# Gate folded into the FFN weights, first batch's keys taken raw out of PSUM, and new engine orders

## The reference

```
mod = silu(c) @ wmod                      # six vectors a batch: sa ca ga sb cb gb
ga, gb = sign * max(|.|, 0.25)
h = layernorm(x) * (1 + ca) + sa
q, k, v = h @ Wqkv + bqkv                 # 256 wide each, one head
x = x + ga * (softmax(q k^T / 16) v @ Wo + bo)
h = layernorm(x) * (1 + cb) + sb
W = weight + lora_B[b] @ lora_A[b]        # combined for each batch
x = x + gb * (h @ W^T + bias)
```

## Time and profile before

| | |
|---|---|
| median of three runs | 1043.1 us |
| the profiled execution, its own time | 1042.57 us |
| its span, first to last instruction | 1040.8 us |
| PE busy | 1011.5 us, 97% |
| DVE, ACT, POOL busy | 663.6, 309.2, 231.2 us |
| mean granted TensorE clock | 0.993 of full |
| read from and written to HBM | 146.25 MB and 33.65 MB |

### The profile page before, as it was taken

The page is one execution under the profiler, slowest core; times in us unless marked ns, Lnnn a source line. Parts: engine busy times, 40 slices in busy tenths (PEclk is TensorE's granted clock), DMA queues, the critical chain, the costliest instruction groups (busy, mean ns, idle before and its releaser), DMA issues.

```text
span 1040.8 us, 12891 instructions
## 1 busy us (share of the span) xinstructions
PE 1011.5 (97%) x5158; PEld 831.6 (80%) x5158; DVE 663.6 (64%) x827; ACT 309.2 (30%) x460; POOL 231.2 (22%) x182
## 2 busy tenths in 40 slices
PE   4899999999999999999999999999999999999996
PEld 1677777888888889888898888888887888888885
DVE  4866756498744398532976548776688578566622
ACT  1422333123232132420234523322432333142300
POOL 0000000423201322004230034342223315042411
PEclk9899999999999999999999999999999999999999
DMA  9987574767102553024443146565553646463421
GB/s 348 409 317 244 211 295 140 252 227 265 70 1 77 207 197 127 1 94 157 155 162 117 41 142 225 203 220 184 200 202 126 216 145 202 140 225 122 142 76 66
DMA packets 54475, 180.74 MB, mean 174 GB/s; under 512 B 5784, under 2 KB 6352, under 8 KB 54416
## 3 DMA queue, kind: packets, MB, share of 16 engines
q1 hardware_dynamic: 45152, 146.35, 40.9%
q0 software_dynamic: 9104, 33.04, 8.4%
q10 hardware_dynamic: 160, 0.53, 0.1%
HBM read 146.25 MB, written 33.65 MB: 173 GB/s over the span
## 4 chain that ended last, share of the span: by engine, by line
PE 91%; DMA 4%; DVE 2%; SPq 1%; issue 1%; POOL 0%; ACT 0%; DVEq 0%; POOLq 0%; ACTq 0%
PE pairC L1370 8%; PE pairA L1370 8%; PE pairC L1371 8%; PE pairC L1372 7%; PE pairA L1371 7%; PE pairA L1372 7%; PE pairD L1370 7%; PE pairD L1371 7%; PE pairD L1372 7%; PE pairB L1370 5%; PE pairB L1371 5%; PE pairB L1372 5%; DMA z_cols<-in_x_cols 2%; PE pairB L1526 1%; PE pairD L1478 1%; PE pairA L1478 1%
## 5 line engine op out<-in xcount | busy, mean ns | idle before, releaser
L923 POOL TENSOR_TENSOR xr<-xr,row_bc 128x1024 f32<-128x1024 f32 x32 | 79.9, 2503 | 110.1 <-DMA xr<-in_x 90.3
L936 POOL TENSOR_TENSOR res<-res,row_bc 128x1024 f32<-128x1024 f32 x32 | 81.7, 2565 | 83.4 <-DMA res<-x_dram 76.9
L1370 PE MATMUL pairC<-w_hi,h_hi 128*128 128x512 f32 (+1 forms) x256 | 90.1, 352 | 0.0
L1371 PE MATMUL pairC<-w_lo,h_hi 128*128 128x512 f32 (+1 forms) x256 | 90.0, 351 | 0.0
L1372 PE MATMUL pairC<-w_hi,h_lo 128*128 128x512 f32 (+1 forms) x256 | 89.6, 350 | 0.0
L1370 PE MATMUL pairD<-w_hi,h_hi 128*128 128x512 f32 (+1 forms) x224 | 77.6, 346 | 0.0
L1371 PE MATMUL pairD<-w_lo,h_hi 128*128 128x512 f32 (+1 forms) x224 | 77.6, 346 | 0.0
L1372 PE MATMUL pairD<-w_hi,h_lo 128*128 128x512 f32 (+1 forms) x224 | 77.2, 345 | 0.0
L928 POOL DMA_DIRECT2D x_dram<-xr x32 | 18.0, 562 | 229.3 <-DVE xr L1276 229.3
L1079 ACT ACTIVATE w_hi<-w_sum 128x1024 fp32r<-128x1024 f32 x32 | 33.8, 1059 | 100.5 <-DVE w_sum L1320 100.2
L1370 PE MATMUL pairB<-w_hi,h_hi 128*128 128x512 f32 (+1 forms) x160 | 59.8, 374 | 0.0
(11 more groups left out here) (344 smaller groups left out, 2570.9 us busy)
## 6 DMA issues: line engine op xcount, KB each, us to landing
wm<-in_wmod SPq DMA_DIRECT2D x48, 512.0 KB, 6.4
xr<-in_x SPq DMA_DIRECT2D x34, 512.0 KB, 4.0
z_cols<-in_x_cols SPq DMA_DIRECT2D x32, 512.0 KB, 6.3
x_dram<-xr POOLq DMA_DIRECT2D x32, 512.0 KB, 3.8
xs<-x_dram SPq DMA_DIRECT2D x32, 512.0 KB, 4.7
w2t<-in_w2t SPq DMA_DIRECT2D x32, 512.0 KB, 4.3
res<-x_dram SPq DMA_DIRECT2D x32, 512.0 KB, 5.7
out_y<-res POOLq DMA_DIRECT2D x31, 512.0 KB, 3.5
```

Source lines behind the costliest of these rows:

```text
L923: nc.gpsimd.tensor_tensor(xt, xt, row_bc[:, :], ALU.add).then_inc(residual_made, 1)
L936: nc.gpsimd.tensor_tensor(rt, rt, row, ALU.add).then_inc(residual2_made, 1)
L1370: nc.tensor.matmul(out, left[0], right[0], start=first, stop=False)
L1371: nc.tensor.matmul(out, left[0], right[1], start=False, stop=False)
```

## The change

Four things are changed.

1. The gate gb is multiplied into the combined weights: a new step `WG` (DVE) multiplies each piece of `w_sum` by the gate in place, between `WS` and `WH2`. `FG` and the buffer `gated` are gone; `FA` adds the PSUM pair straight to `res`, and it is `FA` that frees the pair.
2. The product for the first vector, ca, is cut by output columns and no longer by rows: `M0`, `MC0`, `MT0`, `MM0`, each for two column tiles of h. Each of its eight loads brings 256 columns of 512 rows, in pieces of 1 KB where a whole row of 4 KB was one piece. A new step `V0` makes values in chunks as `K0` does keys.
3. The spread statistics are taken for both halves of the first batch by PE (`BCM` the means, `BCP` the rest), and ACT copies them out of PSUM (`BMC`, `BPC`) into `bc`, where `Z` reads them; before, the second half went through DRAM.
4. Keys of the first batch are copied raw out of PSUM into `k_raw` (`KR`, ACT), and `KH` and `KL` read that. `k_raw` lies where wm tiles lay, so that the second vector's loads have four tiles in turn, not six.

All five tables are new. The core of the diff:

```
-PARTS = ((1, 0), (1, 1), (0, 0), (0, 1), (2, 0), (2, 1))
+PARTS = ((1, 0), (2, 0), (1, 1), (2, 1), (0, 0), (0, 1))
 PE_ORDER:
-    ("BCP", (), "A", None), ("M", (0, 0), "B", None), ("M", (0, 1), "B", None), ("M", (0, 2), "B", None),
+    ("BCM", (0,), "A", None), ("BCP", (0,), "A", None), ("M0", (0,), "B", None), ("MT0", (0,), "B", None),
...
-            elif what == "BCP":
-                eng.wait_ge(z_made, 4)
+            elif what == "BCM":
+                eng.wait_ge(spread_copied, 2 * i[0] + 2)
+            elif what == "K" and i[0] == 0:
+                eng.wait_ge(k_raw_made, 2 * i[1] + 2)
-                eng.wait_ge(y_gated, f_no(*i) + 1)
+                eng.wait_ge(y_made, f_no(*i) + 1)
...
+                    if s == CA:
+                        half, at = k % 2, q * H + k // 2 * 2 * P
+                        src = wmod[half * BANK:(half + 1) * BANK, at:at + 2 * P].rearrange("(k p) n -> p k n", p=P)
+                        sp.dma_start(wm[k].rearrange("p (k n) -> p k n", k=4), src).then_inc(ld_wm[k], 16)
...
+                elif what in ("BMC", "BPC"):
+                    j = i[0]
+                    wait(act, z_made, 4 * j)
+                    nc.scalar.activation(bc[:, cols], ps[:, cols], ACT.Copy).then_inc(spread_copied, 1)
+                elif what == "KR":
+                    _, j, m = i
+                    act.wait_ge(k_done, 2 * j + m + 1)
+                    act.wait_ge(mod_used, 6)
+                    nc.scalar.activation(k_raw[:, m, j * CHUNK:(j + 1) * CHUNK], ps[:, m * BANK:(m + 1) * BANK],
+                                         ACT.Copy).then_inc(k_raw_made, 1)
...
                 elif what == "WH2":
-                    act.wait_ge(w_sum_made, 8 * b + n + 1)
+                    act.wait_ge(w_gated, 8 * b + n + 1)
...
+                elif what == "MM0":
+                    c = i[0]
+                    dve.wait_ge(ca_turned, c + 1)
+                    nc.vector.tensor_scalar(modT[:, PLACE[CA], :, 2 * c:2 * c + 2],
+                                            ps[:, BANK:BANK + 2 * B].rearrange("p (c b) -> p b c", b=B), 1.0, None,
+                                            ALU.add).then_inc(ca_made, 1)
...
-                elif what == "FG":
+                elif what == "WG":
+                    b, n = i
+                    h = n // 4
+                    dve.wait_ge(ld_gate2, 16 * (b + 1))
+                    dve.wait_ge(w_sum_made, 8 * b + n + 1)
+                    wt = w_sum[:, n % 2, :].rearrange("p (c n) -> p c n", c=2)
+                    gate = gate_bc[:, h * BANK:(h + 1) * BANK].unsqueeze(1).to_broadcast([P, 2, BANK])
+                    nc.vector.tensor_tensor(wt, wt, gate, ALU.mult).then_inc(w_gated, 1)
+                elif what == "FA":
+                    dve.wait_ge(residual2_made, n + 1)
-                            nc.vector.tensor_tensor(gated[:, cols], ps[:, cols], gate_bc[:, BANK:2 * BANK],
-                                                    ALU.mult).then_inc(y_half_gated, 1)
-                            nc.vector.tensor_tensor(res[:, slot, cols], res[:, slot, cols], gated[:, cols],
+                            nc.vector.tensor_tensor(res[:, slot, cols], res[:, slot, cols], ps[:, cols],
                                                     ALU.add).then_inc(y_half_made, 1)
                     dve.wait_ge(f_done, n + 1)
-                    gate = gate_bc[:, h * BANK:(h + 1) * BANK].unsqueeze(1).to_broadcast([P, 2, BANK])
-                    nc.vector.tensor_tensor(gated[:, :].rearrange("p (t n) -> p t n", t=2),
-                                            ps[:, :].rearrange("p (t n) -> p t n", t=2), gate, ALU.mult).then_inc(y_gated, 1)
-                    nc.vector.tensor_tensor(res[:, slot, :], res[:, slot, :], gated[:, :], ALU.add).then_inc(y_made, 1)
+                    nc.vector.tensor_tensor(res[:, slot, :], res[:, slot, :], ps[:, :], ALU.add).then_inc(y_made, 1)
...
+                elif what == "M0":
+                    c = i[0]
+                    for k in range(CT):
+                        q = 32 * (k % 4)
+                        last = nc.tensor.matmul(ps[q:q + 32, 0:2 * P], scT[:, k * B:k * B + 32],
+                                                wm[2 * c + k // 4][:, k % 4 * 2 * P:(k % 4 + 1) * 2 * P],
+                                                start=(k < 4), stop=(k >= 4))
...
+                elif what == "V0":
+                    c = i[0]
+                    pe.wait_ge(w_lo_made, PARTS.index((2, c // 2)) + 1)
+                    pe.wait_ge(h0_lo_made, 2 * c + 2)
+                    for ct in range(2 * c, 2 * c + 2):
+                        for t in range(4):
+                            last = product3(ps[:, t * D:(t + 1) * D], both(h_hi[0], h_lo[0], ct, slice(t * P, (t + 1) * P)),
+                                            both(w_hi, w_lo, ct, slice(2 * D, 3 * D)), ct == 0 and t % 2 == 0, ct == CT - 1)
```

More of the change, by code:

```diff
@@ L521, in build_block @@
             with ExitStack() as early:
-                wm = [sb(f"wm{i}", [P, H], at=early) for i in range(4)]
+                wm_pair = [sb(f"wm{i}", [P, 2, H], at=early) for i in range(2)]
             wo_hi = sb("wo_hi", [P, DT, H], F32R, at=first)
@@ L533, in build_block @@
             q_lo = sb("q_lo", [P, DT, S], F32R, at=first)
+            k_hi = sb("k_hi", [P, DT, S], F32R, at=first)
+            with ExitStack() as early:
+                wm_pair += [sb(f"wm{i}", [P, 2, H], at=early) for i in (2, 3)]
+            with ExitStack() as early:
+                k_raw = sb("k_raw", [P, DT, S], at=early)
             k_lo = sb("k_lo", [P, DT, S], F32R, at=first)
-            with ExitStack() as early:
-                wm += [sb(f"wm{i}", [P, H], at=early) for i in (4, 5, 6, 7)]
-            k_hi = sb("k_hi", [P, DT, S], F32R, at=first)
             v_hi = sb("v_hi", [P, QT, D], F32R, at=first)
             v_lo = sb("v_lo", [P, QT, D], F32R, at=first)
+        wm = [wm_pair[i // 2][:, i % 2, :] for i in range(8)]
         wo_raw = [xr, probs, probs, probs]
@@ L961, in step @@
                     act.wait_ge(mod_used, CT * (s + 1))
-                    wait(act, mod_turned, s)
+                    if s == SA:
+                        act.wait_ge(ca_turned, 4)
+                    else:
+                        act.wait_ge(mod_turned, s - 1)
                     if s == GA:
@@ L1229, in step @@
                     dve.wait_ge(hi_made, 4 * b + 2 * j + m + 1)
-                    nc.vector.scalar_tensor_tensor(lo[where], ps[:, m * BANK:(m + 1) * BANK],
+                    src = k_raw[where] if what == "KL" and b == 0 else ps[:, m * BANK:(m + 1) * BANK]
+                    nc.vector.scalar_tensor_tensor(lo[where], src,
                                                    bias_qkv[:, col + m, b:b + 1], hi[where].bitcast(F32),
@@ L1369, in product3 @@
             def product3(out, left, right, first, last):
-                nc.tensor.matmul(out, left[0], right[0], start=first, stop=False)
-                nc.tensor.matmul(out, left[0], right[1], start=False, stop=False)
-                return nc.tensor.matmul(out, left[1], right[0], start=False, stop=last)
+                nc.tensor.matmul(out, left[0], right[0], start=first, stop=False, skip_group_check=True)
+                nc.tensor.matmul(out, left[0], right[1], start=False, stop=False, skip_group_check=True)
+                return nc.tensor.matmul(out, left[1], right[0], start=False, stop=last, skip_group_check=True)
             def both(hi, lo, *where):
@@ L1405, in step @@
                     last.then_inc(mod_turned, 1)
-                elif what == "BCP":
+                elif what in ("BCM", "BCP"):
+                    j = i[0]
                     pe.wait_ge(ld_const, 16)
-                    pe.wait_ge(rstd_made, 1)
-                    for k in range(2):
-                        for t in range(4):
-                            at = k * CHUNK + t * P
-                            last = nc.tensor.matmul(ps[:, at:at + P], stat[:, 0, k, t:t + 1].to_broadcast([P, P]), ident,
-                                                    start=True, stop=True)
-                    last.then_inc(stat_spread, 1)
+                    if what == "BCM":
+                        pe.wait_ge(stat_made, 4 * j + 4)
+                    else:
+                        pe.wait_ge(rstd_made, j + 1)
+                    k = 0 if what == "BCM" else 1
+                    for t in range(4):
+                        at = k * CHUNK + t * P
+                        last = nc.tensor.matmul(ps[:, at:at + P], stat[:, j, k, t:t + 1].to_broadcast([P, P]), ident,
+                                                start=True, stop=True)
+                    last.then_inc(mean_spread if what == "BCM" else stat_spread, 1)
                 elif what == "RT0":
```

167 lines of the change are left out of this document (90 added, 77 removed), and 699 rows, old and new, of tables (ACT_ORDER, DVE_ORDER, PE_ORDER, POOL_ORDER).

## The result

The changed kernel took 1051.41 us (median of four: 1049.35, 1050.78, 1052.05, 1052.26), the kernel before 1042.99 beside it: ratio 1.0084, 95% interval 1.0071 to 1.0097. By the ratio it is 8.8 us slower. The prediction was 1041.5, with a range up to 1046.0: wrong, and on the wrong side.

A forecast was written before the change was run, and what follows sets the result against it. PE was taken as the bound, busy 1011.5 of 1040.8 us. The sum 1042.57 - 4.0 + 3.8 + 0.8 - 0.8 - 0.8 = 1041.6 was stated as 1041.5 us; range for 8 in 10 runs 1036.8 to 1046.0.

The forecast's parts named there:

- the start: From kernel start to the first score: PE gets ahead by the new order; booked -4.0 us, between -5.2 and -3.6.
- the FFN's hole: Beginning of the FFN: PE idles before the first F because DVE's chain to the fifth w_sum is longer; +3.8 us.
- the clock: Behind the hole at the FFN's beginning the clock may be low; half booked, +0.8 us, between 0 and 2.4.
- old waits: PE's waits of 0.6 us for probs and 0.2 behind a gated pair go; -0.8 us, bounds -0.8 and 0.
- the tail: After the last F: one of two 512-column instructions in a row goes; -0.8 us, bounds -0.8 and -0.7.
- the clock's fall at 84: Between Q and the first S: the lower clock, which cost 1.6 us, was expected not to occur in the new order.
- The loads of 1 KB pieces: Eight wm loads for ca: each taken to land 0.2 us later, making Q 1.6 us later.
- the landing of load 29: In the start: LWq(0,0), the 29th load, lands at 42.5 us by formula, and Q(0,0)'s chain begins there.
- the extra spreading: In the start: about 2 us of extra PE work, with 8 thin spreading matmuls, covered by waiting for loads.
- I checked the places where F takes a pair: In the FFN: where F takes a pair from a recent F or W, one to several us are left, except the beginning.
- Rival B: FFN: hole at its upper end with the clock down, similar holes in the next three batches; 1047 us, chance 0.15.

The follow-up runs named there:

- whole rows: Changed kernel with ca's eight wmod loads in 4 KB pieces: ratio 1.0087 to the kernel before; the same on its start with the old rest: 0.9993.
- the second trace of before: The kernel before, unchanged, profiled again on one chip: that execution took 1040.57 us, and its clock did not fall at 84 us.
- the repaired lists: Changed kernel, two GpSimd additions waiting for NM and W(0,7) two sub-steps later: ratio to the kernel before 1.0050 with the gate folded, 1.0013 with FG back.
- the new start with the old lists: Changed tables and code up to score S(1,4), about 270 us, then the kernel before's tables with the gate in FG: ratio 0.9992 to the kernel before.
- the first experiment: Changed kernel with the gate back in FG and no WG, all other rows in the new order: ratio 1.0091 to the kernel before.

## Why the prediction was wrong

The sum had -4.0 for the start, +3.8 for the FFN's hole, +0.8 for the clock, -0.8 for old waits and -0.8 for the tail. By the ratios, the 8.8 us are made up like this, undone one after the other from the changed kernel: 2.6 for the two additions beside NM, 0.9 for W(0,7), 3.9 for the fold (hole, clock and tail), 2.2 for the rest of the new order, less 0.8 for the start. In another order W(0,7) is worth more, and each has some 2 us of noise. Term by term:

- **Start, -4.0: failed.** It measured -0.8 (between -2.0 and +0.4). Its own parts gave -5.2 + 1.6 = -3.6, so 0.4 of the -4.0 had no reason. The 1.6 us for the clock's fall at 84 was read from one execution; it fell in two of three, so it is worth about 1.1. The loads of 1 KB pieces cost 0.25 us each, near the 0.2 I chose; they were not free, so -5.2 was out of reach. What is left, 2.0 to 2.4 us without the clock, came out at 0.1 to 0.4, and two steps failed there. The first is the landing of load 29, on which Q(0,0) hangs: the formula has 42.5, and 44.1 with my price for the pieces, and ACT could start on it at 45.68. With whole rows that was 43.70, so the formula itself was 1.2 us short. The second is the extra spreading, which that landing was to cover. Up to the first score of the second batch (274.8 us) PE is busy for 2.5 us more in the matmuls that spread the statistics than the second trace of before (6.3 and 3.8), 2.8 less on the products with wmod (26.8 and 29.6), and idles 1.4 less behind its first matmul; with some smaller parts that is 1.0 less from its first matmul on, which itself starts 0.9 later. This is read from traces; no run takes the spreading out. I took one start of Q for the measure and multiplied out content; the first score of the second batch is the sum that can be read.
- **The FFN's hole, +3.8: right in mechanism, and near in size.** In the changed kernel the waits under O(3,5) and the first F are 3.2 us. In the repaired lists the fold costs 4.3 us of waiting (1.9 and 2.88 - 0.46), 3.9 with the tail in the time; some 1.6 of it is the meeting of two WG with an addition, which I had only as the upper bound, so the count of instructions alone is nearer to 2.7.
- **The clock behind it, +0.8:** 1.7 in the profiled execution, within the bounds and twice the value taken. Other traces with a hole there have one such stretch, two or none.
- **Old small waits, -0.8: wrong sign.** The wait for probs went, but 0.6 for q_lo, 0.24 and 0.24 came, and with the gate back two of 0.54 behind h_lo. Even repaired, the new lists' kernel stands 2.2 us behind the new start with the old lists (1.0013 against 0.9992, the intervals just overlapping). The waits named here make up less than 2 us of it; the rest is open.
- **Tail, -0.8: right.** From the last matmul to the span's end it takes 1047.5 - 1038.88 = 8.6 us where it took 9.4.
- **What I did not see: GpSimd beside NM, +2.6.** "I checked the places where F takes a pair" was the step that failed: T takes its input from NM, and NM's length hangs on GpSimd's list. At 929 us two additions now follow the rstd at once (RS2(13), R2(2,1,1,0), R2(2,1,1,1)), where one had stood ahead of it. The signs were there: FA's 3.34 us, the pair of NM of 5.71 us in the kernel before, and the rule of the Trainium skill in "VectorE: DVE Perf Modes" (Two Vector instructions with no wait between them), which has instructions in a 2-port mode beside those with two SBUF inputs. I applied it to WG, the new instruction, and not to the old ones whose neighbours had changed.
- **Also unseen: W(0,7) behind X1(3,7)**, 4.1 us without the fold (2.0 of them its wait), hidden by the hole with it (1.0059 and 1.0050). With it in the lists, taking the fold out gives nothing: a wait of 2.07 came for one that fell by 2.4. So the first experiment refuted my reading of the change though not of the hole.

Rival B was the nearest, with its sign right, 1047, and chance 0.15, but not for its reasons, so that its sign is partly luck. The clock was down. The waits from the first W to the first F grew by 4.6 us, between my 3.8 and its 5.4, but 1.4 of them for NM. It had FA long and the weights late in three more batches: FA was never long (1.22 at most), and the late hole was one of T. Its parts also add up to 1048.4 and not 1047. The "places checked" had no mechanism by which a wait could come from a list that isn't PE's or DVE's.

Not settled: why the lead of 1.15 us with whole rows is gone by 274 us, and only 0.4 at the first score in the new start alone (124.27 against 124.62 and 124.66); and what in an execution decides whether the clock falls.

## What to carry to other kernels

When a change rewrites the order of all engines, read pairs of lists and not lists: for each instruction of VectorE with both tensors in SBUF that PE waits for, see what GpSimd does beside it. A wait that is removed shows the next one (2.9 gave way to 2.1), so count the slack of the row behind before booking a gain. A stretch of low clock can be in one execution of a kernel and not in the next, as here in two of three: look at several before booking its price.

## What the runs showed of the hardware

- GpSimd's addition of 128x1024 and an instruction of VectorE with all its large tensors in SBUF (NM, WG, WL2, and FA before the change) do not share time, they take turns for whole instructions: NM 0.8 us alone, a pair 5.64 beside two additions; WL2 1.2 alone, a pair 6.75 beside two; three additions 9.08 where one alone takes 2.39. X1, WS and the changed kernel's FA, with one operand in PSUM, were not stretched (1.28, 1.22 and 1.22 us at most): WS took 1.21 at 623.48 and 624.62, during this addition (POOL's timeline of the changed kernel):

```profile
622.98 2.82 POOL L940 TENSOR_TENSOR xr<-xr,row_bc 128x1024 f32<-128x1024 f32 x1
```

   The page "SBUF — State Buffer" of the Trainium skill (SBUF: two separate sides) says that VectorE and GpSimd share a pair of ports, which one of them holds for its whole instruction; the rows agree. They also agree with its naming instructions in a 2-port mode, since NM has only one large tensor to read and still waits.
- Between 10 and 30 us, with eight loads of 512 KB in pieces of 1 KB among others, the DMA engines moved 376 GB/s, and with these eight in pieces of 4 KB 411; two pairs of kernels show the same two figures.
- The granted clock at one place of one kernel is not the same in every execution: between 80 and 90 us it was 0.83, 0.83 and 1.00 of full in three traces of the old start.
